# One Mamba layer and a routed expert layer on one core: the scan stage's router counts, softplus and round loop rearranged

## What is computed

```python
x_ssm, x_gate = split(x @ in_proj_w.T + in_proj_b)
x_conv = silu(causal_conv_4(x_ssm) + conv_b)
B, C = split(x_conv @ bc_w.T + bc_b)                  # 16 states
dt = softplus(x_conv @ dt_w.T + dt_b)
h  = h * exp(dt * A) + (dt * B) * x_conv              # scan over 512 tokens, per channel and state
y  = (sum over states of h * C + x_conv * D) * silu(x_gate)
z  = layernorm(y @ out_w.T + out_b + x) * ln_g + ln_b
x  = layernorm(x + z)
logits = x @ router_weight.T + router_bias
top-4 of 8, softmax of the four, each token's experts (SwiGLU, 512 wide) summed with these weights
out = layernorm(x + experts)
```

## Time and profile before

| what | value |
|---|---|
| median of 3 runs | 1354.8 us (1353.71 to 1355.67) |
| profiled execution, its own time | 1347.08 us |
| its span in the profile | 1345.2 us |
| mean granted clock of TensorE | 0.943 |
| busy: PE, DVE, ACT, POOL | 1173.2, 1057.6, 896.5, 790.9 us |
| stage 1 | from 0 to about 640 us, rounds 3 to 6 about 72 us each |
| expert tiles and last norm | the rest, to 1345.2 us |

### The profile page before, as it was taken

How to read it: one execution, slowest core, us unless ns; L and a number is a source line. 1 busy time by engine, 2 the same in 40 slices (tenths; PEclk the granted TensorE clock), 3 DMA queues, 4 the chain that set the end, 5 groups by cost and what they waited for, 6 DMA issues and landing times. The chain is left out here.

```text
span 1345.2 us, 18463 instructions
## 1 busy us (share of the span) xinstructions
PE 1173.2 (87%) x5138; PEld 804.4 (60%) x5138; DVE 1057.6 (79%) x1814; ACT 896.5 (67%) x1551; POOL 790.9 (59%) x566
## 2 busy tenths in 40 slices
PE   7879797979979797786899999999999999999940
PEld 3324252534334343334788888888888888888840
DVE  2999999999999999993867677776677776767734
ACT  4775949495857767526667667777677777766734
POOL 0557568889888888997634444344444433444442
PEclk9999899998989898876999999999999999999985
DMA  2543434445354545426865565665566666556537
GB/s 96 212 158 126 174 117 176 167 164 194 125 205 145 185 151 190 163 80 248 343 153 136 146 166 159 161 162 140 133 157 162 162 161 159 134 135 166 160 38 250
DMA packets 69260, 217.19 MB, mean 161 GB/s; under 512 B 7520, under 2 KB 43232, under 8 KB 56288
## 3 DMA queue, kind: packets, MB, share of 16 engines
q1 hardware_dynamic: 29664, 167.42, 34.1%
q0 software_dynamic: 26880, 36.72, 16.1%
q10 hardware_dynamic: 12672, 12.58, 2.9%
HBM read 165.54 MB, written 51.15 MB: 161 GB/s over the span
## 5 line engine op out<-in xcount | busy, mean ns | idle before, releaser
L649 PE MATMUL p_y<-read,small 128*128 128x512 f32 x512 | 269.6, 664 | 67.6 <-POOL read L1185 67.6
L1049 DVE TENSOR_TENSOR_SCAN state<-decay,p_bu 128x512 f32<-128x512 f32 x256 | 297.2, 1202 | 6.8 <-ACT decay L830 5.1
L1507 POOL DMA_INDIRECT total<-o_v,tok x144 | 266.1, 1848 | 44.8 <-issue 44.8
L649 PEld LDWEIGHTS p_y<-read,small 128*128 128x128 f32 x512 | 103.3, 210 | 215.8 <-issue 108.3
L1505 POOL TENSOR_TENSOR scrap<-neg_half 128x1 f32<-128x1 f32 x36 | 13.7, 379 | 318.1 <-ACT o_v L1414 310.4
L830 ACT ACTIVATE decay<-dt,scan_rate 128x511 f32<-128x511 f32 x256 | 164.7, 710 | 15.4 <-DVE state L1049 15.1
L1185 POOL TENSOR_TENSOR read<-state,bc 128x1024 f32<-128x1024 f32 x64 | 149.9, 2352 | 27.7 <-DVE p_bu L1040 9.9
L513 ACT ACTIVATE gate_v<-p_g,bias 128x512 f32<-128x512 f32 x144 | 98.4, 684 | 101.2 <-PE p_up L503 100.7
L1227 POOL DMA_INDIRECT queues<-rows,index x128 | 134.3, 1049 | 32.5 <-issue 28.6
L1401 ACT ACTIVATE ah<-a_v 128x512 fp32r<-128x512 f32 x144 | 91.1, 633 | 90.7 <-DVE a_v L527 90.7
L521 DVE TENSOR_SCALAR up_v<-up_v 128x512 f32<-128x512 f32 x144 | 61.3, 426 | 64.9 <-ACT up_v L516 64.9
(11 more groups left out here) (222 smaller groups left out, 3015.7 us busy)
## 6 DMA issues: line engine op xcount, KB each, us to landing
bc<-bc_rows SPq DMA_DIRECT2D x32, 1024.0 KB, 4.9
first_raw<-in_w_experts SPq DMA_DIRECT2D x19, 1668.0 KB, 7.0
raw_w<-in_w_experts SPq DMA_DIRECT2D x18, 1668.0 KB, 6.8
first_wh<-bc_rows SPq DMA_DIRECT2D x16, 1024.0 KB, 5.0
first_wl<-bc_rows SPq DMA_DIRECT2D x16, 1024.0 KB, 4.6
first_rows<-queues SPq DMA_DIRECT2D x19, 544.0 KB, 6.9
xq<-queues SPq DMA_DIRECT2D x18, 544.0 KB, 6.9
queues<-pad SPq DMA_DIRECT2D x9, 544.0 KB, 11.7
```

The lines of the kernel that those rows point to most:

```text
L649: mm = pe.matmul(p_y[h][:, :], ident[:, :], read[:, t % 4, h, :], start=False, stop=(t == SLOTS - 1))
L1049: dve.tensor_tensor_scan(state[t % 4][:, h, :], decay[t % AHEAD][:, h, :], p_bu[:, h * LEN:(h + 1) * LEN], 0.0, ALU.mult, ALU.add).then_in ...
L1507: pool.indirect_dma_start(total, bass.IndirectOffsetOnAxis(ap=tok[t.p][:, a:a + 1], axis=0), o_v[t.p][:, a, :], None, compute_op=ALU.add). ...
```

## The change

Four things in stage 1, and one in the set-up.

1. **Counts ahead of the output projection.** TensorE does `count` in slot 3 ahead of `project_out`, where it was in slot 4 behind it; VectorE takes the counts in slot 3 instead of 5. Round 9 keeps its places. The block `cnt` stands ahead of `o0`, `o1` in the order of banks.
2. **Two decays between the softplus' parts.** ScalarE's `softplus` is cut in two: exp and 1 + exp in slot 9, the log in slot 10 behind the decays of states 11 and 12 (round -1 keeps both together). VectorE adds the log in slot 12 (`add_log`) instead of 11. GpSimd's read of slot 11 waits for `s_rest`, that of slot 12 for `s_sum`; one scatter moves from slot 11 to slot 12.
3. **Rank by one difference and one comparison.** The five operations become a subtraction of all pairs and a comparison with a mask that holds 0 or -2^-126.
4. **Rounds written out.** The hardware loop over rounds 3 to 6 goes, in all engines; no wait counts in a register any more there.
5. One more small operation in the set-up scales the mask.

```diff
@@ Round.blocks
-        return (["tr0", "tr1", "rt"] * d + ["in0", "in1"] * a + ["o0", "o1"] * c + ["cnt"] * d + ["cv0", "cv1"] * a
+        return (["tr0", "tr1", "rt"] * d + ["in0", "in1"] * a + ["cnt"] * d + ["o0", "o1"] * c + ["cv0", "cv1"] * a
@@
-def rounds(eng):
-    lo, hi = Round.LOOP.start, Round.LOOP.stop
-    for i in range(Round.FIRST, lo):
-        yield Round(Seq(0, i), i)
-    with eng.Fori(lo // 2, hi // 2) as half:
-        for off in range(2):
-            yield Round(Seq(half, lo % 2 + off), lo + off)
-    for i in range(hi, Round.LAST + 1):
-        yield Round(Seq(0, i), i)
+ROUNDS = [Round(Seq(0, i), i) for i in range(Round.FIRST, Round.LAST + 1)]
@@ TensorE
+                if r.d and t == (4 if r.last else 3):
+                    count(r)
                 if r.c and t == 3:
                     project_out(r, 0)
                     project_out(r, 1)
-                if r.d and t == 4:
-                    count(r)
@@ ScalarE
                 if r.a and t == 9:
-                    softplus(r)
+                    softplus_exp(r)
                     if r.like == Round.FIRST:
+                        softplus_log(r)
...
                     decays(r.s.at(1), t - SLOTS + AHEAD - 2)
+                if r.a and r.b and t == 10:
+                    softplus_log(r)
@@ VectorE
-            dve.tensor_tensor(cmp[:, 0, :, :, :], other, own, ALU.is_ge)
-            yield from steps.step(dve.tensor_tensor(cmp[:, 1, :, :, :], other, own, ALU.is_gt))
-            dve.tensor_tensor(cmp[:, 0, :, :, :], cmp[:, 0, :, :, :], lower[:, :, :].unsqueeze(1).broadcast_to([P, TT, E, E]), ALU.mult)
-            yield from steps.step(dve.tensor_tensor(cmp[:, 1, :, :, :], cmp[:, 1, :, :, :], upper[:, :, :].unsqueeze(1).broadcast_to([P, TT, E, E]), ALU.mult))
-            yield from steps.step(dve.tensor_tensor(cmp[:, 0, :, :, :], cmp[:, 0, :, :, :], cmp[:, 1, :, :, :], ALU.add))
+            yield from steps.step(dve.tensor_tensor(cmp[:, :, :, :], other, own, ALU.subtract))
             dve.tensor_reduce(top[:, :], lg[:, :, :], AX.X, ALU.max)
-            yield from steps.step(dve.tensor_reduce(rank[:, :, :], cmp[:, 0, :, :, :], AX.X, ALU.add))
+            yield from steps.step(dve.tensor_tensor(cmp[:, :, :, :], cmp[:, :, :, :],
+                                                    lower[:, :, :].unsqueeze(1).broadcast_to([P, TT, E, E]), ALU.is_gt))
+            yield from steps.step(dve.tensor_reduce(rank[:, :, :], cmp[:, :, :, :], AX.X, ALU.add))
@@
-                if r.d and t == 5:
+                if r.d and t == (5 if r.last else 3):
                     take_counts(r, route_steps)
@@
                 if r.a and t == (11 if r.b else 10):
                     softplus_rest(r)
+                if r.a and t == (12 if r.b else 10):
+                    add_log(r)
@@ GpSimd
-        SCATTERS = {9: (0, 1), 11: (2, 3, 4), 13: (5, 6), 15: (7, 8)}
+        SCATTERS = {9: (0, 1), 11: (2, 3), 12: (4,), 13: (5, 6), 15: (7, 8)}
@@
             if r.a and t == 11:
+                pool.wait_ge(s_rest, r.s.at(1).n + 1)
+            if r.a and t == 12:
                 pool.wait_ge(s_sum, r.s.at(1).n + 1)
```

More of the change, by code:

```diff
@@ L56 @@
     FIRST, LAST = -1, SEQS + 1
-    LOOP = range(3, SEQS - 1)
     def __init__(self, seq, like):
@@ L77, in block @@
         k = start + self.blocks().index(name)
-        turns = 0 if isinstance(self.s.half, int) else self.s.half - Round.LOOP.start // 2
-        return k % 2, k // 2 + 1 + len(self.blocks()) * turns
-def rounds(eng):
-    lo, hi = Round.LOOP.start, Round.LOOP.stop
-    for i in range(Round.FIRST, lo):
-        yield Round(Seq(0, i), i)
-    with eng.Fori(lo // 2, hi // 2) as half:
-        for off in range(2):
-            yield Round(Seq(half, lo % 2 + off), lo + off)
-    for i in range(hi, Round.LAST + 1):
-        yield Round(Seq(0, i), i)
+        return k % 2, k // 2 + 1
+ROUNDS = [Round(Seq(0, i), i) for i in range(Round.FIRST, Round.LAST + 1)]
 def constants():
@@ L274, in build @@
     logp = x1t
-    cmp = sb("cmp", 2, TT, E, E, at=one)
+    cmp = sb("cmp", TT, E, E, at=one)
     pone = ctx.enter_context(ExitStack())
@@ L304, in build @@
     s_residual = sem("s_residual")
-    ROUTE_STEPS = 13
+    ROUTE_STEPS = 12
+    SMALLEST = 2.0 ** -126
     first_loads = [(w[:, k, 0:DT_], ins["weights"][k, :, 0:DT_]) for k in range(KD)]
@@ L698, in count @@
             mm.then_inc(done, 1)
-        for r in rounds(pe):
+        for r in ROUNDS:
             for t in range(SLOTS):
@@ L714, in pe_stage1 @@
                     project(r, 1)
+                if r.last and t == 4:
+                    up_projection(pe, Seq(0, 0), 1)
+                if r.d and t == (4 if r.last else 3):
+                    count(r)
                 if r.c and t == 3:
@@ L717, in pe_stage1 @@
                     project_out(r, 1)
-                if r.last and t == 4:
-                    up_projection(pe, Seq(0, 0), 1)
-                if r.d and t == 4:
-                    count(r)
                 if r.a and t == 4:
@@ L799, in store_dt, with softplus_exp @@
             act.activation(expo[:, h, :], bank[:, :], ACT.Abs, bias=b_dt[:, h:h + 1]).then_inc(done, 1)
-        def softplus(r):
+        def softplus_exp(r):
             s = r.s.at(1)
@@ L809, in softplus, with softplus_log @@
             act.activation(flat(rest[:, :, :]), flat(expo[:, :, :]), ACT.Identity, bias=1.0).then_inc(s_t, 1)
+        def softplus_log(r):
             if r.d:
@@ L884, in router_exp @@
             act.activation(flat(ex[:, :, :]), flat(ex[:, :, :]), ACT.Exp).then_inc(s_rexp, 1)
-        for r in rounds(act):
+        for r in ROUNDS:
             for t in range(SLOTS):
@@ L987, in dve_setup_rest @@
         dve.tensor_copy(base[:, :], c_queue[:, :])
+        dve.tensor_scalar(lower[:, :, :], lower[:, :, :], -SMALLEST, None, ALU.mult)
         dve.tensor_copy(before[:, :], c_before)
@@ L1014, in softplus_rest, with add_log @@
                                      ALU.add, ALU.subtract).then_inc(s_rest, 1)
+        def add_log(r):
+            s = r.s.at(1)
             dve.wait_ge(s_log, s.n + 1)
@@ L1121, in dve_stage1 @@
         plan = plan_early(dve, plan_steps)
-        for r in rounds(dve):
+        for r in ROUNDS:
             for t in range(SLOTS):
@@ L1257, in release_rows @@
             pool.tensor_tensor(scrap[:, 2:3], neg_half[:, 0:1], neg_half[:, 0:1], ALU.mult).then_inc(s_left, 1)
-        for r in rounds(pool):
+        for r in ROUNDS:
             for t in range(SLOTS):
```

## The result

| kernel | median | lowest to highest | profiled execution | its span |
|---|---|---|---|---|
| before | 1354.3 us (4 runs) | 1352.8 to 1355.7 | 1347.1 | 1345.2 |
| changed | 1346.1 us (4 runs) | 1345.2 to 1347.8 | 1347.8 | 1345.9 |

The changed kernel is **8.2 us faster**: 0.994 of before, interval 0.9926 to 0.9953. The forecast was 1334.3, range 1327 to 1342: the direction is right, the size is not. They are compared here by stretches; a second profile of each kernel follows among the experiments.

The account below looks back on a forecast made before the run. VectorE bound the kernel, GpSimd close behind; after the change GpSimd's 66.2 us plus waits set 68.0 us rounds. Savings 4.75 + 16.8 + 1.5, together 23.0, less 2.6 lost in round 8: 20.5 off 1354.8, 1334.3 us, range 1327 to 1342.

Parts of the forecast that it names:

- Up to round 2: Stretch through round 2's softplus: GpSimd has room, VectorE's savings count whole, one softplus 2.7, one rank 1.15, counts 0.9: 4.75 us.
- Steady round: Rounds 3 to 6: GpSimd's 66.2 us plus waits make 68.0 a round, bounds 67.3 and 70; 16.8 us saved.
- Rank 1.15: VectorE's rank: from 2.15 us to 1.0, saving 1.15 us in each of eight rounds.
- softplus 2.4: VectorE, product of slot 11 to its scan: 2.4 us less at most in each of rounds 1 to 6.
- counts 0.9: VectorE's wait for TensorE's counts: 0.9 us saved in round 2, bounds 0.1 and 1.4.
- turn 1.6: Turn of the round loop: VectorE waited 2.28 us, the stage paid 1.6, taken as wholly saved.
- Counts, rounds 3 to 6: VectorE's remaining wait for the counts, 0.3 to 1.3 us in slot 3, held to lie inside the 68.0.
- round 6's end: GpSimd's read in round 6 starts about 6.8 instead of 8.3 us after slot 11's product: 1.5 us saved.
- The hold in round 8: TensorE waits for `chosen` at the counts, output projection 2.7 us late: 2.6 us lost, bounds 0 and 2.7.
- Rival 2: VectorE's softplus addition and GpSimd's read block each other each round: 8.5 us saved, 1346; at half, 1340; chance 0.15.
- Rival 3: Code of the written-out rounds comes late, stopping engines 2.28 us per fresh stretch; twelve stalls give 1361.7; chance 0.03.
- rival 1: VectorE stays the bound, GpSimd catches up, round 8's hold is hidden: 27.5 us saved, 1327.3; chance 0.12.

Follow-up runs that it names:

- second pair of profiles: Changed kernel and the one before, both unaltered, run and profiled again: 1343.31 us (0.9938) and 1354.36 us (1.0001).
- Experiment 3: Changed kernel with one of GpSimd's 16 scatters of a round moved from slot 13 to slots 2 and 3 of the next round: 1335.0 us, 0.9895 of before.
- experiment 2: Changed kernel with ScalarE's second variance ahead of slot 11's evacuation and decays instead of behind them: 1338.62 us, 0.9905 of before.
- experiment 5: Changed kernel with one part undone at a time; ratios to before: counts 0.9951, softplus in one piece 0.9968, rank by two comparisons 0.9951, loop back 0.9927.

## Why the prediction was wrong

- **Up to round 2**: 4.75 forecast. The first three spacings of `p_u` give 0.1, 1.9 and 3.0 in the second pair of profiles: 5.0 (5.7 in the first pair). The size is right.
- **Steady round**: 68.0 forecast, 70.1 measured. This is the step that failed: rounds 3 to 6 gave 8.4 us, not 16.8. The bound was taken as a sum, GpSimd's 66.2 plus the wait for `z`, with the sentence that its other waits "vanish as it falls behind". They don't: beside 62.40 of work, 4.1 of issue, 1.53 for `z` and 0.50 for the addition GpSimd waits 1.51 in the round of 70.07 for ScalarE's second variance, a term that the forecast put at nothing. Of before, the 1.99 at 511.80 was a wait for VectorE that hid one for ScalarE, whose variance was done at 513.71, only 0.4 ahead of the power. Experiment 3 shows that the sum is not the bound, experiments 2 and 3 that the loop is.
- **Rank 1.15, softplus 2.4, counts 0.9, turn 1.6**: as durations on VectorE they came (the rank's chain is 1.02, no wait for decays, 0.16 for the log, 1.20 for the counts, no turn). As time of the kernel they are 0 to 1.5, 4.0, 1.5 and nothing (rank, counts and turn within the intervals). Rank and turn are worth least, since VectorE's wait for the counts, 1.2 us, takes up what they would cost.
- **Counts, rounds 3 to 6**: the forecast held the remaining wait for harmless. It is, at 1.2; at 2.9 it is a microsecond a round.
- **Behind the rounds**: 1.5 forecast for round 6's end and 0.7 measured. The hold in round 8 was foreseen (3.03 for 2.7), its price not: 5.4 instead of 2.6 (gate to residual, both pairs of profiles), since the clock after it was no term of the sum. The terms measured are 5.0 + 8.4 + 0.7 - 5.4 = 8.7, beside the 8.2 of the result.
- **Rival 2** (addition and GpSimd's read block each other): no addition is over 1.23 us. The block was real but elsewhere, in `p_u` (2.73) and in the first residual (1.26 for 0.42). The rule cited there, the Trainium skill, SBUF — State Buffer, section "SBUF: two separate sides", agrees with what was seen: `p_u` has both inputs in SBUF and waits for the read's end, `p_bu`, of which one input is in PSUM, lasts 1.27 beside the same reads. The stretch of `p_u` cost nothing by itself, as experiment 5 shows; in experiment 2 it went but for 0.1. That rival 2 names 1346 and 1346.1 was measured is chance: its additions were never blocked.
- **Rival 3** (late code): no new stop on any engine's rounds; experiment 5 shows the opposite question answered, that the loop cost nothing.
- The signs named in the forecast worked: 70.1 between starts of `p_u` and GpSimd's waits show at once that neither the forecast's 68.0 nor rival 1 holds.

## What to carry to other kernels

When an engine that is busy 94% gets faster, don't look for the next busiest engine but for the next longest *loop*: start at an instruction, follow releasers through every engine until the same instruction of the next round, and add the legs and their slacks. Here it was 70.2 of 71.8 in a trace that showed no engine but VectorE above 90%, and once known it gave moves of a few lines each that together were worth more than the change. A move that is good in the steady rounds should be taken back in the last one, where nothing covers it; and a matrix engine that has to stand can cost more than the time it stands, here 5.3 us for 3.0.

## What the runs showed of the hardware

- A pause of 3.03 us of TensorE was followed by some 5 us at the granted clock of 0.50; without the pause the clock was 1.00 in the same stretch.
- GpSimd's indirect DMA takes 0.96 to 1.11 us in most places of a round, but 1.80 where VectorE's `p_u` runs beside it (514.35 above), in both kernels.
- The turn of the hardware loop stopped VectorE for 2.28 us in one kernel and for 0.78 in another, with the same bounds.
- The same kernel differs by some 7 us between chips (before: medians 1347.1 to 1354.4), and in the runs whose chip is on record either every profile of a chip has the unexplained wait of VectorE in round 9 or none has.
